# Two bias products taken out of a fused attention and router kernel: a constant feature carries them, prepared by accumulating DMAs during attention

## What is computed

```python
x = x + attention(layernorm(x), ctx, Wq, Wkv, Wout)        # causal, 16 heads of 32
h = layernorm(x).reshape(T, H)                              # T = 4096 tokens, H = 512
logits = (h @ router_w.T + router_b).reshape(T, O, E)       # O = 512 outputs, E = 8 experts
probs = softmax(logits, axis=-1)
w, sel = top_k(probs, 2);  w = w / w.sum(-1, keepdims=True)
c = zeros((T, E)).at[t, sel].add(w)                         # summed over the outputs
expert_out = einsum('th,eoh->teo', h, expert_w) + expert_b
x = x + einsum('te,teo->to', c, expert_out)
```

## Time and profile before

| | us |
|---|---|
| median of three runs | 2065.03 |
| the profiled execution, its own time | 2067.4 |
| its span | 2065.6 |
| TensorE busy, share of the span | 1986.0 (96%) |
| VectorE busy | 1451.6 (70%) |
| ScalarE busy | 1046.7 (51%) |
| GpSimd busy | 854.5 (41%) |

### The profile page before, as it was taken

The page is one execution under the profiler, slowest core; times in us unless marked ns, Lnnn a source line. Parts: engine busy times, 40 slices in busy tenths (PEclk is TensorE's granted clock), DMA queues, the critical chain, the costliest instruction groups (busy, mean ns, idle before and its releaser), DMA issues.

```text
span 2065.6 us, 31279 instructions
## 1 busy us (share of the span) xinstructions
PE 1986.0 (96%) x9994; PEld 1532.4 (74%) x10044; DVE 1451.6 (70%) x3010; ACT 1046.7 (51%) x2093; POOL 854.5 (41%) x987
## 2 busy tenths in 40 slices
PE   5899999999987999999999999999999999999999
PEld 3667677676754777777777777778888888888887
DVE  5677767766656577777777777478787788787532
ACT  2666566556534367767677677544333344333300
POOL 3687777777666235344353543212111132111100
PEclk8999999999998999999999999999999999999999
DMA  5455454554453545454554544553222223222110
GB/s 158 119 129 136 125 140 126 136 148 119 124 185 123 205 154 183 162 208 163 192 181 152 206 175 187 201 186 112 87 76 87 86 89 110 87 76 85 52 41 31
DMA packets 99218, 275.84 MB, mean 134 GB/s; under 512 B 13435, under 2 KB 14480, under 8 KB 95030
## 3 DMA queue, kind: packets, MB, share of 16 engines
q1 hardware_dynamic: 94518, 216.16, 33.0%
q10 hardware_dynamic: 4608, 58.72, 8.3%
HBM read 131.67 MB, written 92.27 MB: 108 GB/s over the span
## 4 chain that ended last, share of the span: by engine, by line
PE 86%; DVE 5%; DMA 2%; POOL 2%; issue 2%; ACT 1%; SPq 1%; ACTq 0%; DVEq 0%; POOLq 0%
PE pair L265 21%; PE pair L267 21%; PE pair L266 21%; PE pair L636 3%; PE pair L669 3%; PE ps L682 3%; PE ps L265 3%; PE ps L266 3%; PE ps L267 3%; PE pair L880 2%; DVE pair L1312 1%; SPq L371 1%; PE ps L702 1%; DVE nmax L1306 1%; ACT pT L1044 1%
## 5 line engine op out<-in xcount | busy, mean ns | idle before, releaser
L265 PE MATMUL pair<-w_h,hT 128*128 128x512 f32 x1920 | 797.1, 415 | 3.5 <-DVE xb L1644 1.9
L267 PE MATMUL pair<-w_h,hT 128*128 128x512 f32 x1920 | 751.7, 392 | 0.0
L266 PE MATMUL pair<-w_l,hT 128*128 128x512 f32 x1920 | 747.6, 389 | 0.0
L1837 POOL TENSOR_TENSOR logits<-logits,second 128x512 f32<-128x512 f32 x224 | 298.3, 1367 | 609.1 <-DVE second L1523 608.8
L267 PEld LDWEIGHTS pair<-w_h,hT 128*128 128x128 f32 x1920 | 360.6, 188 | 80.2
L266 PEld LDWEIGHTS pair<-w_l,hT 128*128 128x128 f32 x1920 | 361.6, 188 | 74.7
L265 PEld LDWEIGHTS pair<-w_h,hT 128*128 128x128 f32 x1920 | 363.3, 189 | 71.4 <-issue 2.3
L1644 DVE SCALAR_TENSOR_TENSOR xb<-pair,c_now,xb 128x512 f32<-128x512 f32 x256 | 191.9, 750 | 190.4 <-PE pair L267 183.2
L1044 ACT ACTIVATE pT<-pair,zero 128x1024 f32<-128x1024 f32 (+3 forms) x256 | 202.5, 792 | 203.1 <-PE pair L669 200.2
L1312 DVE CUSTOM_DVE_ANT_0 pair<-pair,future 128x256 f32<-128x256 f32 (+3 forms) x340 | 184.3, 554 | 128.7 <-PE pair L636 121.1
L636 PE MATMUL pair<-qk_st 96*128 96x256 f32 (+3 forms) x512 | 160.9, 344 | 22.0 <-DVE nmax L1312 11.4
(11 more groups left out here) (171 smaller groups left out, 2847.8 us busy)
## 6 DMA issues: line engine op xcount, KB each, us to landing
logits<-lg_all ACTq DMA_DIRECT2D x32, 1792.0 KB, 7.9
qk_st<-qk SPq DMA_DIRECT2D x384, 128.0 KB, 2.3
lg_all<-ev_a SPq DMA_DIRECT2D x32, 768.0 KB, 6.4
lg_all<-ev_b SPq DMA_DIRECT2D x32, 768.0 KB, 3.3
xb<-x SPq DMA_DIRECT2D x64, 256.0 KB, 3.0
hT_all<-hT SPq DMA_DIRECT2D x32, 512.0 KB, 3.6
hT<-hT_all SPq DMA_DIRECT2D x32, 512.0 KB, 3.8
xt<-in_x SPq DMA_DIRECT2D x8, 1024.0 KB, 5.4
```

The lines of the kernel that those rows point to most:

```text
L265: pe.matmul(dst, lh, rh, start=start, stop=False)
L266: pe.matmul(dst, lh, rl, start=False, stop=False)
L267: return pe.matmul(dst, ll, rh, start=False, stop=stop)
L1837: pool.tensor_tensor(logits[t % 2][:, e - 1, :], logits[t % 2][:, e - 1, :], second[:], ALU.subtract)\
```

## The change

The first of the 512 normalised features is set to 1 (GpSimd, in `deviation`), and the normalisation writes only features 1 to 511. The normalised features of a token sum to 0, so the first is minus the sum of the others: its weight row, subtracted from all the rows, makes it superfluous, and row 0 is then free for the bias. Fifteen matrices of this form (seven router differences and eight experts) are made in DRAM (`w_fix`) during the attention. SyncE copies one matrix a group from the inputs (`copy_weight`, groups 1 to 15, 1 MB each); GpSimd adds to it with accumulating DMAs (`sum_weight`, one a group at step 4, groups 2 to 23): minus matrix 0 for the router (`whole`, 1 MB), and minus the first row, broadcast to 512 rows. Both engines wait for the one before. At the start of the last batch SyncE writes the bias rows over row 0 (`put_biases`).

The bias products of the router, the selector, the bias parts, the differences on VectorE and GpSimd, and all of c's padding, turning and multiplying go away. In the last batch ScalarE issues the loads of six router matrices; it rounds three at (1,7), (2,5), (2,7), and VectorE makes their low parts at (2,6), (3,0), (3,2). In the epilogue `divided` and `scaled` of the last group come first on VectorE, and GpSimd's last `lo_outputs` before `deviation`.

```diff
+            sp.dma_start(neg_base[:], routerT[:, 0, :].rearrange("(c p) o -> p c o", p=P)).then_inc(s["prep_in"], 16)
+            sp.dma_start(own_row[0:ND, :], routerT[0, 1:NE, :]).then_inc(s["prep_in"], 16)
...
+                    if first and c == FIX_COPIED:
+                        sp.wait_ge(s["prep_ok"], 4)
+                        sp.dma_start(base_neg.rearrange("(c p) o -> p c o", p=P), neg_base[:]).then_inc(s["prep_out"], 16)
...
+                    if FIX_COPIED <= n < FIX_COPIED + ND + NE:
+                        copy_weight(n - FIX_COPIED)
+
+            def copy_weight(k):
+                if k:
+                    sp.wait_ge(s["fix_copy"], k * 16)
+                src = routerT[:, k + 1, :] if k < ND else expertT[:, k - ND, :]
+                sp.dma_start(w_fix[k], src).then_inc(s["fix_copy"], 16)
+
+            def put_biases():
+                sp.wait_ge(s["fix_sum"], FIX_SUMS * 16)
+                sp.dma_start(w_fix[0:ND, 0, :], rows_bias).then_inc(s["fix_rows"], 16)
+                sp.dma_start(w_fix[ND:ND + NE, 0, :], expert_b).then_inc(s["fix_rows"], 16)
...
+            def sum_weight(j):
+                k, whole = (j // 2, j % 2 == 0) if j < 2 * ND else (j - ND, False)
+                if j == 0:
+                    pool.wait_ge(s["prep_out"], 64)
+                else:
+                    pool.wait_ge(s["fix_sum"], j * 16)
+                pool.wait_ge(s["fix_copy"], (k + 1) * 16)
+                if whole:
+                    pool.dma_start(w_fix[k].rearrange("(p a) o -> p (a o)", p=P),
+                                   base_neg.rearrange("(p a) o -> p (a o)", p=P), accum_op=ALU.add,
+                                   max_dma_last_dim=8192).then_inc(s["fix_sum"], 16)
+                else:
+                    pool.dma_start(w_fix[k], rows_neg[k:k + 1, :].broadcast_to([H, O]), accum_op=ALU.add)\
+                        .then_inc(s["fix_sum"], 16)
...
+                        if v == FIX_STEP and FIX_SUMMED <= n < FIX_SUMMED + FIX_SUMS:
+                            sum_weight(n - FIX_SUMMED)
...
-                    pe.matmul(bank, bias_sel[:, k, :], bias_rows[:], start=True, stop=False)
                     for c in range(KC):
                         mm = three(pe, bank, hT_h[i][:, c], hT_l[i][:, c], w_h[:, k, c, :], w_l[:, k, c, :],
-                                   False, c == KC - 1)
+                                   c == 0, c == KC - 1)
...
-                pe.transpose(c_ps[:, 0:P], c_pad[i][:], ident[:]).then_inc(s["cT_mm"], 1)
-                pe.matmul(b_ps[:], cT[i][:], eb[:], start=True, stop=True).then_inc(s["cb_mm"], 1)
...
+            act.wait_ge(s["prep_in"], 6 * 16)
+            act.activation(neg_base[:], neg_base[:], ACT.Copy, scale=-1.0).then_inc(s["prep_ok"], 1)
...
+                        if last and (c, v) in FIXED:
+                            load_router(FIXED.index((c, v)))
+                        if last and (c, v) in HI_EARLY:
+                            hi_router(HI_EARLY.index((c, v)))
...
             def epilogue():
-                dve.wait_ge(s["shifted"], NB * UNITS)
-                dve.memset(bias_rows[:], 0.0).then_inc(s["bias_zero"], 1)
+                divided(NB - 1, KC - 1)
+                scaled(NB - 1, KC - 1, last_o_ps)
                 stats2(0, 0)
                 mean_variance(0, 0, "ln2")
-                lo_router(0)
+                lo_router(3)
                 norm2(0, 0)
-                divided(NB - 1, KC - 1)
-                scaled(NB - 1, KC - 1, last_o_ps)
-                lo_router(1)
                 lo_block(0, 0)
...
-                    dve.tensor_tensor(xb[i][:], b_ps[:], xb[i][:], ALU.add).then_inc(s["acc"], 1)
...
             def deviation(g, slot, name):
                 pool.wait_ge(s[name + "_var"], g + 1)
+                if name == "ln2":
+                    pool.memset(xb[slot][:, 0:1], 1.0).then_inc(s["one_ok"], 1)
...
             def epilogue():
                 lo_outputs(NB - 2, KC - 2)
-                deviation(0, 0, "ln2")
                 lo_outputs(NB - 1, KC - 1)
+                deviation(0, 0, "ln2")
```

More of the change, by code:

```diff
@@ L218, in build @@
         names += [f"raw{e}_in" for e in range(NE)]
-        names += [f"diff{e}_in" for e in range(NE)]
+        names += [f"fix{k}_in" for k in range(ND)]
         s = {n: sem(n) for n in names}
@@ L399, in body @@
                     n = b * KC + c
+                    if c == 0 and not more:
+                        put_biases()
+                    if c == 0 and b == 1:
+                        sp.wait_ge(s["prep_out"], 64)
                     if c == 0 and more:
@@ L1072, in epilogue @@
                 hi_outputs(NB - 2, KC - 2, B - 1)
-                for k in range(4):
+                for k in range(len(HI_EARLY), 4):
                     hi_router(k)
@@ L1149, in normed @@
                 act.wait_ge(s["ln2_nb"], t - 1)
-                act.activation(xb[i][:], xb[i][:], ACT.Identity, scale=rstd[:, i:i + 1], bias=nbias[:, i:i + 1])\
+                act.activation(xb[i][:, 1:H], xb[i][:, 1:H], ACT.Identity, scale=rstd[:, i:i + 1],
+                               bias=nbias[:, i:i + 1])\
                     .then_inc(s["hn_ok"], 1)
@@ L1189, in route @@
                         hi_block(t + 1, 1 - i)
-                    if t == 0 and k == 4:
-                        act.wait_ge(s["eb_in"], 48)
-                        act.activation(eb[:], eb_raw[:], ACT.Copy).then_inc(s["eb_hi"], 1)
                     if t == 1 and k == 0:
@@ L1779, in body @@
                             split_context(b + 1)
-                        if not more and (c, v) in SELECTED:
-                            select_bias(SELECTED.index((c, v)))
+                        if v == FIX_STEP and FIX_SUMMED <= n < FIX_SUMMED + FIX_SUMS:
+                            sum_weight(n - FIX_SUMMED)
                         if (c, v) in SPLIT and not (first and c == 0):
@@ L1786, in body @@
                             scales(b + 2, STATISTICS.index((c, v)))
-            SELECTED = ((1, 0), (1, 2), (1, 4), (2, 0))
-            def select_bias(step):
-                if step == 0:
-                    for pair in range(2):
-                        pool.wait_ge(s[f"stacked{pair}"], NB * (16 * STACK_DMAS))
-                    pool.memset(bias_sel[:], 0.0).then_inc(s["sel_z"], 1)
-                else:
-                    pool.wait_ge(s["sel_z"], 1)
-                    if some(step - 1):
-                        pool.wait_ge(s["sel_ok"], step - 1)
-                    pool.affine_select(out=bias_sel[:], in_=bias_sel[:], compare_op=ALU.not_equal, fill=1.0,
-                                       base=(1 - step) * ND, pattern=[[-1, ND], [0, P]], channel_multiplier=1)\
-                        .then_inc(s["sel_ok"], 1)
             def epilogue():
                 lo_outputs(NB - 2, KC - 2)
+                lo_outputs(NB - 1, KC - 1)
                 deviation(0, 0, "ln2")
-                lo_outputs(NB - 1, KC - 1)
             for b in range(B):
```

246 lines of the change are left out of this document (75 added, 171 removed).

## The result

The changed kernel takes 2185.5 us (median of 4 runs, 2182.8 to 2187.1) against 2066.4 of the kernel before beside it: ratio 1.0576, 95% interval 1.0557 to 1.0594, so 119 us slower. The forecast was 2015 us, with a range of 1988 to 2052.

What follows compares the result with a forecast made beforehand. TensorE was taken to bound the kernel, holding 86% of the chain of waits. From the profiled 2067.4 us, terms summing to -50.4 and 2.4 down to the median gave 2014.6, say 2015 us; 8 in 10 for 1988 to 2052.

Steps and rivals of the forecast that it cites:

- `rows` delayed by the sums: Attention: each of 22 sums delays the small `rows` transfer 0.7 us past its slack, +15.4 us, 0 to +75.
- C: Rival: DMA engines fill in attention, groups 2 to 15 lose 2 to 4 us each; 2033 to 2073 us; 13%.
- D: Rival: a sum takes longer than a group, GpSimd's queue waits for the one before; 2133 us at 28 us each; 8%.
- B: Rival: sums hide in attention, `rows` keeps its slack; cost 0 to 10 us, 1988 to 1998 us; 15%.
- E: Rival: ScalarE or VectorE limits the shorter router block, half the 51.5 us gain lost; 2041 us; 4%.
- GpSimd's time: Attention: issuing a sum takes GpSimd 2.0 us, 0.8 covered by slack, in six groups; +7 us, 0 to +19.
- Router: Router stage: 224 bias products fall away from TensorE's queue at 0.230 us each, -51.5 us.
- (d): First router block: stall of about 2 us for weights 4 to 6 that GpSimd had to subtract goes, -2.2 us.
- Last batch and epilogue: Last attention batch and epilogue: shorter waits less ScalarE's new roundings, net -16.0 us, between 0 and -22.
- (a): Last batch: 6.11 us wait for row maxima behind router loads in SyncE's queue goes, with slow clock behind, -8.1 us.
- (b): Last batch: waits of 4.46 and 4.16 us for GpSimd shrink as VectorE's weight subtractions go, -2.0 and -3.8 us.
- (c): Epilogue: 4.01 us wait for the last group's `lo_outputs` goes, with slow products behind it, -5.6 us.

Runs made afterwards that it cites:

- run 1: Changed kernel without GpSimd's 22 accumulating DMAs and the wait for them, the 15 weight copies kept: 1989.3 us, ratio 0.9625 to the kernel before.
- run 2: Changed kernel with the 22 sums as plain copies that add nothing: issued by GpSimd 2135.8 us, issued by ScalarE 2118.0 us.
- run 8: Changed kernel with sums in lines of 1 KB, 2110.8 us, or 512 B, 2107.3; 1 KB lines also in a kernel with router sums halved, 2033.3.
- run 9: Changed kernel without the sums, ScalarE issuing the last batch's six router loads at one step instead of one by one: 1990.2 us.

## Why the prediction was wrong

The sum of the trace: 2065.6 - 61.0 (router) - 7.0 (experts) - 15.3 (last batch and epilogue) + 3.0 (copies and preparation) + 197.0 (sums) + 2.4 (before group 2, and groups 24 to 27) = 2184.7. The span is 2184.8.

**`rows` delayed by the sums: +15.4 forecast, +197.0 measured.** This is the step that failed. I took 0.7 us past the slack "since the two share engines and not a queue". Runs 1, 2 and 8 show that a small transfer issued behind a large one waits for lines of the large one, whichever queue that one is on: `nm_l` landed 5 to 10 us late, and PE stood 2.9 to 9.9 us for it in each of 21 groups, where 0.7 was forecast. Behind GpSimd's sums of many lines it waits for a part of them, behind ScalarE's transfer for all. The upper bound, 3.6 us, came from the landing of a plain 1 MB load, while a sum takes 9.1 or 14.8; it was no bound. And I priced a microsecond of waiting as one: 149.1 us of standing drew 47.9 us of slower clock behind them. The idle share of the DMA engines (0.49) said nothing of how long one transfer waits: in the wait shown above they were busy for 0.96 of it. (During `stack`, too, they are not "nearly full": 0.70 in the 8.07 us read there.)

**Rivals.** Of the prediction's rivals C had the cause nearest (the sum across `stack` and `rows`), with 2 to 4 us in groups 2 to 15; it was nothing in group 2 and 4.7 to 13.9 us in each of 3 to 23, with a copy in the group or not. D did not happen: a sum takes 14.8 us, less than a group, and GpSimd never stood at step 4 but for the first. B falls by the measured time, E by the router stage below. The slower side, 0.09, I had left mainly to D, while it was C's mechanism, three times as strong, that led there.

**GpSimd's time: +7 forecast, about 0.** The issue takes 0.86 us (8 KB lines) and 1.06 (2 KB) at the median, not 2.0, and PE waits for GpSimd for 1.5 us in all of 60 to 700 us. The fit of the Trainium skill ("DMA: Bandwidth & Descriptors", section "Anatomy of one DMA — SWDGE (gpsimd) path") gave, as an estimate, 4.4 or 6.8 us for the transfer. The trace's 9.1 and 14.8 decide; the plain copy of run 2, 5.0, is near it.

**The first sum: +4 forecast.** GpSimd stood 5.4 us up to 111.75, where 6 was forecast. Group 2 is 17.5 us long in place of 15.4, but it is 17.5 without the sums too: the copy and the preparation do that, the wait is hidden.

**Router: -51.5 forecast, -61.0 measured**, of which some 2 are the stall (d), rightly named: PE's two waits there, 1.6 and 0.4 us, are gone. One block, by the transposes in it, before and after:

```profile
912.60 0.60 PE L857 MATMUL ps<-ident,xb 128*128 128x128 f32 x4
933.96 0.60 PE L857 MATMUL ps<-ident,xb 128*128 128x128 f32 x4
```

```profile
1095.70 0.60 PE L860 MATMUL ps<-ident,xb 128*128 128x128 f32 x4
1115.23 0.60 PE L860 MATMUL ps<-ident,xb 128*128 128x128 f32 x4
```

21.36 us against 19.53, so 1.83 for seven products: a bias product cost 0.26, not a thirteenth of 2.99. The first matmul behind it took 0.58 us in place of 0.40; that the change of data type does this is a guess that no run tests. 32 x 1.83 = 58.6. DVE and ScalarE kept up (PE busy for all 624.7 us), rival E falls.

**Experts: -9.3 forecast, -7.0 measured.** The stall behind DVE grew to 5.4 us where giving back 2.5 meant 4.4; the other 1.3 us I can't place.

**Last batch and epilogue: -13.8 forecast (without the stall counted above), -15.3 measured, by two errors that cancel.** Term (a), -8.1, came to nothing: the wait for `nm_l` fell only from 6.1 to 4.1 us, and groups 28 and 29 together took 42.7 us before and after. The rule of the Trainium skill that I had set aside ("DMA: Bandwidth & Descriptors", section "Issuing engines are not separate DMA queues") would have left (a) out. The trace agrees with it in the length of the groups, and run 9 takes away the reason that I had against it, the spreading. From group 30 to the first router product it was 60.7 us before and 45.4 now: -15.3 where (b), (c) and ScalarE's roundings made -5.7. For the +5.7 of the roundings the stretches show no sign; no run takes them out. The two waits for GpSimd fell from 8.6 to 4.6 us, and that for `lo_outputs` is gone.

**Hidden edits: 0 forecast, +3.0**, 2.1 of them in group 2.

## What to carry over

Ask of a large background transfer not how busy the DMA engines are but what small transfer is issued behind it and when that is needed, at both of its ends: the reader of its destination and the next writer of its source. Look also for transfers whose landing the issuing queue awaits before it sends the small one. Where there is such a one, cut the large transfer so that a piece fits in the gap ahead of it, or move it to a stage whose critical engine reads nothing fresh from a DMA; shorter lines helped the small one through behind GpSimd's sums, although they lengthened these. Count a wait inside a stretch at full clock for more than its length, here by a third (47.9 on 149.1 us) and more.

## What was unexpected of the hardware

- An accumulating DMA of 1 MB in DRAM took 9.1 us with lines of 8 KB (5.0 as a plain copy), the row form 10.0, 14.8, 16.6 and 18.5 with lines of 8 KB, 2 KB, 1 KB and 512 B, and GpSimd's issue of a row's sum 0.86, 1.06, 2.35 and 2.83 us at the median for 128, 512, 1024 and 2048 lines.
- Lines of 1 KB and 512 B in place of 2 KB made the sum slower and the kernel faster: `nm_l` landed after 6.8, 4.7 and 1.9 us at the median.
- Behind GpSimd's sum lines of `rows` went out in its midst, behind ScalarE's plain transfer of as many lines only at its end (`nm_l` landed 0.5 to 1.1 us after it in the ten groups where it was issued within 5 us).
- The issue of a small DMA itself is held up behind a large one: `nm_l` took SyncE 1.66 us at 560.02 in place of 0.59, and five loads of 1 MB held ScalarE for 10.6 us.
- With a wait of 2.9 to 9.9 us in each group the granted clock was 0.85 over 594 us, and the same 2612 matmuls took 428 us in place of 380.
